# Experts' pass: tokens and silu product transposed in 32x32 blocks on VectorE, with the product moved through DRAM

## The reference, cut to what matters

```python
logits = x @ gate_weight.T                      # 4096 tokens, 64 experts
scores = softmax(logits); topk_w, topk_idx = top_k(scores, 8); topk_w = topk_w / sum(topk_w)
sorted_tokens = repeat(x, 8)[argsort(flat_ids)]           # 32768 rows
g = ragged_dot(sorted_tokens, w_gate, group_sizes)        # 1024 -> 384
u = ragged_dot(sorted_tokens, w_up, group_sizes)          # 1024 -> 384
out = ragged_dot(silu(g) * u, w_down, group_sizes)        # 384 -> 1024
y = sum(out[inv].reshape(-1, 8, 1024) * topk_w[:, :, None], axis=1)
```

## Time and profile before

| | |
|---|---|
| median of 3 runs | 6763.86 us (6763.16 to 6765.04) |
| profiled execution | 6763.85 us, its span 6762.0 us |
| granted TensorE clock, mean | 0.992 |
| TensorE busy over the span | 6614.3 us, 98% |
| DVE, ACT, POOL busy | 3302.4, 2933.3, 1147.4 us |
| DMA packets, bytes | 733960, 1048.19 MB |
| tiles of the experts' pass; expert weight loads in it | 287; 63 of each kind |

### The profile page before, as it was taken

One profiled execution on the slowest core, in us unless ns is written; L12 is line 12 of the kernel. 1 busy time (PEld: TensorE's weight loads), 2 busy tenths in 40 slices (PEclk: granted clock), 3 DMA queues, 4 the chain that ended last, 5 costly groups with the idle time before them and its releaser, 6 DMA issues.

```text
span 6762.0 us, 107799 instructions
## 1 busy us (share of the span) xinstructions
PE 6614.3 (98%) x34530; PEld 5884.0 (87%) x34531; DVE 3302.4 (49%) x4252; ACT 2933.3 (43%) x3606; POOL 1147.4 (17%) x1015
## 2 busy tenths in 40 slices
PE   9999998999999999699999999999999999999998
PEld 7888887887888788599989999999999999999998
DVE  4443324999999899732443334322422323323333
ACT  3321224888888644432443334322422333333333
POOL 1000000000000155511211211111111212111121
PEclk9999999999999999899999999999999999999999
DMA  8853555555555666455676566654644556556555
GB/s 257 231 197 143 155 143 145 129 127 128 128 129 128 182 171 171 128 156 130 178 211 172 152 174 189 160 137 106 186 106 106 134 134 162 148 147 162 155 153 152
DMA packets 733960, 1048.19 MB, mean 155 GB/s; under 512 B 301281, under 2 KB 531425, under 8 KB 733858
## 3 DMA queue, kind: packets, MB, share of 16 engines
q0 software_dynamic: 109792, 368.12, 23.5%
q1 hardware_dynamic: 467680, 381.55, 22.1%
q10 hardware_dynamic: 156386, 297.29, 13.0%
HBM read 724.43 MB, written 322.31 MB: 155 GB/s over the span
## 4 chain that ended last, share of the span: by engine, by line
PE 51%; DMA 4%; issue 1%; ACT 1%; DVE 1%; ACTq 0%; SPq 0%; POOLq 0%; DVEq 0%
PE moe_ps_y L1332 5%; PE moe_ps_gate L1345 5%; PE moe_ps_gate L1346 5%; PE moe_ps_gate L1347 5%; PE moe_ps_up L1347 5%; PE moe_ps_up L1346 5%; PE moe_ps_up L1345 5%; PE moe_ps_y L1334 5%; PE moe_ps_y L1333 5%; DMA out<-moe_y,moe_rec_s 2%; PE moe_ps_xT L1322 2%; PE moe_ps_hT L1353 1%; DMA moe_rec_s<-table 1%; DMA first_raw<-in_w_up 1%; ACT moe_gu_hi L1375 0%
## 5 line engine op out<-in xcount | busy, mean ns | idle before, releaser
L1449 DVE SCALAR_TENSOR_TENSOR moe_hidden<-moe_silu,moe_rec_w,moe_ps_up 128x384 f32<-128x384 f32 x286 | 175.8, 615 | 1384.6 <-PE moe_ps_up L1347 1190.3
L1345 PE MATMUL moe_ps_gate<-moe_gu_hi,moe_xT_hi 128*128 128x384 f32 x2288 | 793.4, 347 | 11.1 <-DVE moe_xT_lo L1442 7.5
L1300 POOL DMA_INDIRECT out<-moe_y,moe_rec_s x287 | 478.2, 1666 | 1909.9 <-DMA moe_rec_s<-table 1037.5
L1346 PE MATMUL moe_ps_gate<-moe_gu_lo,moe_xT_hi 128*128 128x384 f32 x2288 | 768.1, 336 | 0.0
L1347 PE MATMUL moe_ps_gate<-moe_gu_hi,moe_xT_lo 128*128 128x384 f32 x2288 | 767.8, 336 | 0.0
L1347 PE MATMUL moe_ps_up<-moe_gu_hi,moe_xT_lo 128*128 128x384 f32 x2288 | 765.1, 334 | 0.0
L1345 PE MATMUL moe_ps_up<-moe_gu_hi,moe_xT_hi 128*128 128x384 f32 x2288 | 764.2, 334 | 0.0
L1346 PE MATMUL moe_ps_up<-moe_gu_lo,moe_xT_hi 128*128 128x384 f32 x2288 | 764.2, 334 | 0.0
L1332 PE MATMUL moe_ps_y<-moe_d_hi,moe_hT_hi 128*128 128x512 f32 x1722 | 696.5, 404 | 3.0 <-DVE moe_hT_lo L1455 3.0
L1334 PE MATMUL moe_ps_y<-moe_d_hi,moe_hT_lo 128*128 128x512 f32 x1722 | 677.2, 393 | 0.0
L1333 PE MATMUL moe_ps_y<-moe_d_lo,moe_hT_hi 128*128 128x512 f32 x1722 | 669.6, 389 | 0.0
(11 more groups left out here) (202 smaller groups left out, 13975.2 us busy)
## 6 DMA issues: line engine op xcount, KB each, us to landing
first_raw<-in_w_gate ACTq DMA_DIRECT2D x63, 1536.0 KB, 9.6
first_raw<-in_w_up ACTq DMA_DIRECT2D x63, 1536.0 KB, 14.7
moe_raw_d<-in_w_down ACTq DMA_DIRECT2D x63, 1536.0 KB, 7.1
proj_a_raw<-in_ctxT POOLq DMA_DIRECT2D x64, 512.0 KB, 5.1
kst<-proj_o SPq DMA_DIRECT2D x256, 128.0 KB, 2.7
vst<-proj_o SPq DMA_DIRECT2D x64, 512.0 KB, 2.6
qst<-proj_o SPq DMA_DIRECT2D x256, 128.0 KB, 2.2
att_kt<-kst SPq DMA_DIRECT2D x64, 512.0 KB, 3.6
```

The source lines that it names most:

```text
L1300: nc.gpsimd.indirect_dma_start(out=acc[:, :], out_offset=bass.IndirectOffsetOnAxis(ap=rec_s[:].bitcast(I32)[:, 0:1], axis=0), in_=y[:], in ...
L1345: nc.tensor.matmul(o[:, 0:I], xT_hi[:, c], gu_hi[:, b, k, c], start=(c == 0), stop=False)
L1346: nc.tensor.matmul(o[:, 0:I], xT_hi[:, c], gu_lo[:, b, k, c], start=False, stop=False)
```

## The change

TensorE's transposes go. In their place:
- The output pass writes the features of `h2st` in another order, by quarters (`by_quarter`), and the gate table is loaded to match, in 8 pieces of 32 partitions.
- `rec_g` is loaded four times (one DMA per 32 partitions), POOL makes row numbers of quarter rows from it (`rows`), and four indirect DMAs fetch 1 KB quarters, such that VectorE's transpose in 32x32 blocks (`turn_tokens`, into PSUM) leaves the tokens of t+2 transposed. Gathers run one tile further ahead.
- `hidden` is stored to DRAM (`hst`) and loaded back with four DMAs in another order (`hidden_g`), and DVE transposes it in blocks (`turn_hidden`). The rows of w_down are loaded to match, by four DMAs for each expert.
- DVE's eight splits of gate and up stand in two halves, with `turn_hidden` between them. SP's list has another order. ACT's `tokens_high` waits for gate and up of the tile before, which share its buffer.

The diff, cut to its core:

```diff
+W = 32
+G = P // W
 ...
+def grouped(rows, s):
+    n = rows.shape[1] // G
+    return rows[:, s * n:(s + 1) * n, :].rearrange("o (j a) i -> a (o j) i", a=W)
 ...
+def in_chunks(rows):
+
+    return rows.rearrange("p (j s a) -> p j s a", s=G, a=W)
+
+
+def by_quarter(rows):
+
+    return rows.rearrange("p (s j a) -> p j s a", s=G, a=W)
 ...
-                for dst, src in ((gamma_sb, row_broadcast(gamma, H)), (beta_sb, row_broadcast(beta, H)),
-                                 (gate_sb, gateT.rearrange("(c p) e -> p c e", p=P))):
+                for dst, src in ((gamma_sb, row_broadcast(gamma, H)), (beta_sb, row_broadcast(beta, H))):
                     pool.dma_start(dst[:], src).then_inc(consts_in, 16)
+                gate_rows = gateT.rearrange("(c s a) e -> c a s e", s=G, a=W)
+                for c in range(C):
+                    rows = slice(c % G * W, (c % G + 1) * W)
+                    pool.dma_start(gate_sb[rows].rearrange("a (s h) e -> a h s e", s=G)[:, c // G], gate_rows[c]).then_inc(consts_in, 16)
 ...
-                        nc.scalar.activation(h2[:, 1 - b], x1[:, 1 - b], ACT.Identity, bias=shift[:],
+                        nc.scalar.activation(by_quarter(h2[:, 1 - b]), in_chunks(x1[:, 1 - b]), ACT.Identity, bias=shift[:],
                                              scale=rstd[:, 1]).then_inc(h2_done, 1)
 ...
-        tokens, xT_hi, xT_lo = s.sb("tokens", [P, H], F32R), s.sb("xT_hi", [P, C, P], F32R), s.sb("xT_lo", [P, C, P], F32R)
+        tokens, xT_hi, xT_lo = s.sb("tokens", [P, H]), s.sb("xT_hi", [P, C, P], F32R), s.sb("xT_lo", [P, C, P], F32R)
 ...
+        rec_g, rec_w, rec_s = s.sb("rec_g", [P, G, 2]), s.sb("rec_w", [P, 2]), s.sb("rec_s", [P, 2])
+        group, rows = s.sb("group", [P, 1]), s.sb("rows", [P, G], I32)
+        hidden_g = s.sb("hidden_g", [P, G, I // G])
+        gate_ps, up_ps, hT_ps = s.ps("gate", [P, HALF]), s.ps("up", [P, HALF]), s.ps("hT", [P, G * P])
+        turned, y_ps = s.ps("turned", [P, H]), s.ps("y", [P, H])
+        xT_ps = turned[:].rearrange("p (g j b) -> p j g b", g=G, b=W)
+        hT_t = hT_ps[:, 0:I]
+        hT_v = hT_t.rearrange("p (g j b) -> p j g b", g=G, b=W)
+
+        def by_group(tile):
+            return tile[:].rearrange("p j (g b) -> p j g b", b=W)
 ...
+        h2_quarters = h2st.rearrange("t (s n) -> (t s) n", s=G)
 ...
+                def record_groups(rows):
+                    for k in range(G):
+                        sp.dma_start(rec_g[k * W:(k + 1) * W], rows.rearrange("(g b) w -> b g w", b=W)).then_inc(rec_g_in, 16)
+
+                record_groups(table[REGION:REGION + P, :])
 ...
+                for k in range(G):
+                    sp.dma_start(raw_d[k * W:(k + 1) * W], grouped(w_down[0:1], k)).then_inc(raw_in[2], 16)
 ...
                 def tile(t, is_first=False):
+                    sp.wait_ge(hidden_done, t + 2)
+                    sp.wait_ge(hidden_in, 16 * G * (t + 1))
+                    sp.sem_inc(sp_passed, 1)
+                    sp.dma_start(hst[:, :], hidden[:]).then_inc(hidden_stored, 16)
+                    record(rec_w, t + 1, rec_w_in)
                     if not is_first:
                         sp.wait_ge(added, 16 * t)
                     sp.sem_inc(sp_passed, 1)
                     record(rec_s, t - 1, rec_s_in)
-                    sp.wait_ge(hidden_done, t + 2)
+                    sp.wait_ge(hidden_stored, 16 * (t + 2))
+                    sp.wait_ge(hT_done, t + 1)
                     sp.sem_inc(sp_passed, 1)
-                    record(rec_w, t + 1, rec_w_in)
-                    sp.wait_ge(gathered, 16 * (t + 3))
+                    for k in range(G):
+                        part = hst[:, k * (I // G):(k + 1) * (I // G)].rearrange("(g b) n -> b g n", b=W)
+                        sp.dma_start(hidden_g[k * W:(k + 1) * W], part).then_inc(hidden_in, 16)
+                    sp.wait_ge(rows_done, t + 4)
                     sp.sem_inc(sp_passed, 1)
-                    record(rec_g, t + 3, rec_g_in)
+                    record_groups(record_rows(t + 4))
 ...
-                    pool.wait_ge(rec_g_in, 16 * (t + 1))
-                    pool.wait_ge(xT_done, t)
+                    pool.wait_ge(rec_g_in, 16 * G * (t + 1))
+                    pool.wait_ge(turned_done, t)
                     pool.sem_inc(pool_passed, 1)
-                    nc.gpsimd.indirect_dma_start(
-                        out=f32(tokens[:]), out_offset=None, in_=h2st[:, :],
-                        in_offset=bass.IndirectOffsetOnAxis(ap=rec_g[:].bitcast(I32)[:, 0:1], axis=0)).then_inc(gathered, 16)
+                    nc.gpsimd.tensor_scalar(rows[:], rec_g[:].bitcast(I32)[:, :, 0], float(G), group[:], ALU.mult, ALU.add).then_inc(rows_done, 1)
+                    pool.wait_ge(rows_done, t + 1)
+                    pool.sem_inc(pool_passed, 1)
+                    for g in range(G):
+                        nc.gpsimd.indirect_dma_start(
+                            out=tokens[:, g * (H // G):(g + 1) * (H // G)], out_offset=None, in_=h2_quarters,
+                            in_offset=bass.IndirectOffsetOnAxis(ap=rows[:, g:g + 1], axis=0)).then_inc(gathered, 16)
 ...
+                gather(2)
                 with pool.Fori(0, last_tile + 1) as t:
-                    gather(t + 2)
+                    gather(t + 3)
                     add(t - 1)
 ...
-                def transpose_tokens(t):
-                    pe.wait_ge(gathered, 16 * (t + 1))
-                    for c in range(C):
-                        last = nc.tensor.transpose(xT_r[:, c], tokens[:, c * P:(c + 1) * P], ident_r[:])
-                    last.then_inc(xT_done, 1)
 ...
-                    transpose_tokens(t + 1)
                     down(t - 1, b_before)
-                    pe.wait_ge(hidden_done, t + 2)
-                    for c in range(CI):
-                        last = nc.tensor.transpose(hT_ps[:, c], hidden[:, c * P:(c + 1) * P], ident[:])
-                    last.then_inc(hT_done, 1)
                     if e is not None:
                         pe.wait_ge(w_lo_done, PIECES * e + PIECES)
 
-                transpose_tokens(0)
 ...
                 def tokens_high(t):
-                    act.wait_ge(xT_done, t + 1)
-                    nc.scalar.copy(xT_hi[:], xT_ps).then_inc(xT_hi_done, 1)
+                    act.wait_ge(turned_done, t + 1)
+                    if not (isinstance(t, int) and t == 0):
+                        act.wait_ge(gu_done, 2 * t)
+                    nc.scalar.copy(by_group(xT_hi), xT_ps).then_inc(xT_hi_done, 1)
 ...
-                    act.dma_start(raw_d[:], w_down[bass.ds(e, 1)].rearrange("o (c p) i -> p (o c) i", p=P)).then_inc(raw_in[2], 16)
+                    for s in range(G):
+                        act.dma_start(raw_d[s * W:(s + 1) * W], grouped(w_down[bass.ds(e, 1)], s)).then_inc(raw_in[2], 16)
 ...
                     act.wait_ge(hT_done, t + 2)
-                    nc.scalar.copy(hT_hi[:], hT_ps).then_inc(hT_hi_done, 1)
+                    nc.scalar.copy(by_group(hT_hi), hT_v).then_inc(hT_hi_done, 1)
 ...
                 def tokens_low(t):
                     dve.wait_ge(xT_hi_done, t + 1)
-                    nc.vector.tensor_tensor(xT_lo[:], xT_ps, f32(xT_hi[:]), ALU.subtract).then_inc(xT_lo_done, 1)
+                    nc.vector.tensor_tensor(by_group(xT_lo), xT_ps, f32(by_group(xT_hi)), ALU.subtract).then_inc(xT_lo_done, 1)
+
+                def turn_tokens(t):
+                    dve.wait_ge(gathered, 16 * G * (t + 1))
+                    if not (isinstance(t, int) and t == 0):
+                        dve.wait_ge(xT_lo_done, t)
+                    nc.vector.transpose(turned[:], tokens[:]).then_inc(turned_done, 1)
+
+                def turn_hidden(t):
+                    dve.wait_ge(hidden_in, 16 * G * (t + 2))
+                    dve.wait_ge(hT_lo_done, t + 1)
+                    nc.vector.transpose(hT_t, hidden_g[:].rearrange("p g n -> p (g n)")).then_inc(hT_done, 1)
 
                 def tile(t, e=None, b=None):
                     dve.wait_ge(silu_done, t + 1)
                     dve.wait_ge(gu_done, 2 * t + 2)
-                    dve.wait_ge(hT_done, t + 1)
+                    dve.wait_ge(hidden_stored, 16 * (t + 1))
                     dve.wait_ge(rec_w_in, 16 * (t + 1))
                     nc.vector.scalar_tensor_tensor(out=hidden[:], in0=silu[:], scalar=rec_w[:, 1:2], in1=up_ps[:, 0:I],
                                                    op0=ALU.mult, op1=ALU.mult).then_inc(hidden_done, 1)
                     tokens_low(t + 1)
+                    turn_tokens(t + 2)
                     if e is not None:
-                        split(e, b, 0, GU)
+                        split(e, b, 0, GU // 2)
+                    turn_hidden(t)
+                    if e is not None:
+                        split(e, b, GU // 2, GU)
                     dve.wait_ge(hT_hi_done, t + 1)
```

(4 more changed lines are left out.)

52 lines of the change are left out of this document (24 added, 28 removed).

## The result

| | before | after |
|---|---|---|
| median, range | 6764.45 us, 6763.16 to 6767.01 | 7408.72 us, 7403.17 to 7412.49 |
| span of the profiled execution | 6762.0 us | 7401.6 us |
| granted TensorE clock, mean | 0.992 | 0.947 |

The changed kernel is slower: ratio 1.0951, 95% interval 1.0933 to 1.0968 (four executions of each). The prediction had 6965 us and a range to 7190, so it had the side right and was 444 us too low.

What follows compares the result with a forecast made beforehand. The prediction took TensorE's queue to bound the experts' pass (busy 3877.41 of 3917 us). From 6763.9 us it took 278 for removed transposes and added 479 for waits around 63 weight loads: 6965 us, range 6650 to 7190.

Steps and rivals of the forecast that it cites:

- b: Down product after an expert's first tile: hT_lo comes late, TensorE waits 2.0 us per weight load (0.5 to 3.5).
- c: Second tile of an expert: store and loads of `hidden` land late beside weight loads, delaying down by 2.0 us (1 to 4).
- What is removed: TensorE's token and product transposes and the lateness behind them: 0.97 us saved a tile, 278 us (253 to 298).
- What lies beside TensorE: Added work off TensorE: DVE transposes of 1.15 and 0.5 us, four POOL gathers holding 5.1 us, more SP and ACT transfers.
- Bytes hardly grow: DMA traffic of the added stores, loads and gathers: claimed to hardly grow in bytes.
- The ordinary tile: Tile without weight loads, 12.52 us: the product's trip over two tiles ends at 31.8, wanted at 33.4, 1.6 us to spare.
- a: First tile of an expert: w_down splits and loads delay silu and xT_lo; 4.1 us worked out, 3.6 taken (1.5 to 5).
- The clock: TensorE in the experts' pass: read at a granted clock of 1.00, the 2.4 GHz level; no slow work was added.
- Rival 1: Faster: the product's path is 2.5 us shorter; a, b and c shrink to 3.0 us in all; 6675 us, chance 0.25.
- Rival 2: The path exceeds TensorE's work in every tile, 1.1 us too many in each of 161 tiles; 7142 us, chance 0.12.
- Rival 3: Four turns: beside weights each of four `hidden` loads waits 6.1 us, c is 6.5 us; 7248 us, chance 0.07.

Runs made afterwards that it cites:

- e10: Changed kernel, but SP stores the product, waits, and stores it again before it is loaded: 7736.14 us.
- e5: Changed kernel, but ACT issues the w_down loads in the next expert's first tile, behind silu and the tokens' high part: 7229.78 us.
- e6: Changed kernel, but SP loads the product back before it waits for the sum of t-2 and loads rec_s: 7415.64 us.
- e12: Changed kernel, the product stored only once, in the very first tile; loads bring that old product to every tile, so the output differs: 7304.54 us.
- e13: Changed kernel with e12 and e6 together, neither store nor sum ahead of the product's loads; output is e12's: 7060.88 us.
- e3: Changed kernel without the weight loads of experts 1 to 63; all compute with expert 0's weights, splits stay: 6830.45 us.

## Why the prediction was right or wrong

**The miss in its own terms.** 6965 had 278 saved and 479 lost. Measured are 294 saved, 641 lost by waits and 292 by slow work behind them: 162 + 292 - 16 = 438 us of the 444; the profiled execution lies 6 us under the median. So two steps failed. The slow work is a term that the sum put at nothing, without a reason. And down's waits, b and c together, were priced at 252 us and are 375.3. With the waits as measured and no slow work the time would have been 7127 us, inside the range.

**What is removed: right.** 1.03 us a tile for 0.97. The lateness of the product after each transpose went too, nearly all of the 1.04.

**What lies beside TensorE: nearly right.** DVE's transposes take 1.26 and 0.59 us for 1.15 and 0.5. The gathers start 1.27 us apart, as forecast from the earlier trace rows. "Bytes hardly grow" was wrong: 114 MB more, in 349 thousand more packets.

**The ordinary tile: right.** Forecast were the sum at 6.1 us into the tile and hT_lo ended at 6.8. In the tile from 4295.29 the sum is issued at 4301.40, at 6.1, and hT_lo ends at 4302.48, at 7.2, with 1.2 us to spare instead of 1.6. What the forecast of this tile lacks is the product's own loop of one tile, which has 1.5 us to spare here and which e10 closes.

**a: the mechanism right, the total by luck.** Forecast were the splits' end at 10.7, silu at 13.8 and the next gate product at 16.6 if all of it holds; the rows have 11.2, 14.6 and 17.3. I then took 3.6 for the 4.1 that was worked out, on the ground that ACT can read w_down earlier. The reason helped nothing, since silu stands behind ACTq's loads, which stand behind DVE's splits. Here a is 4.85 us, 4.70 of them the wait. Over all experts the gate products' waits for xT_lo are 267.0 us less the 40.0 at the start of the pass, 227 in all, and 3.6 x 63 is 227. That is luck: 57 experts have a second tile, and there the wait is 4.0 us, the 4.1 that was worked out. Behind the six experts of one tile the gate product waits for splits instead, 35.7 us in all, which was not forecast. e5 confirms the path: with the load moved, first tiles are 3.4 us shorter.

**b: the wait low, the tile wrong.** In this expert down waits 1.74 us for a forecast of 2.0; over all it waits 163 us in 57 second tiles, 2.9 each. And this tile is 4.9 us too long, since its gate product runs at half clock behind a's wait, 2.7 us.

**c: the term that was mis-sized most.** The prediction put the store's and the loads' lateness on down's wait with 2.0 us. Measured are 212 us in 56 waits, 3.8 each. In this expert the third tile is 8.5 us too long: down waits 5.89 and then runs slowly. "The store and the loads of `hidden` fall into that stretch and land 2 to 4 us late each" was right singly (loads 6.01 us for 1.98). Wrong was to price them as one delay on a path with some spare. In this expert nothing was spare, and down waited until 4356.82 for the trip. And there are two ways to the product's loads, the store's landing and the gathers with the sum, that both stretch beside weight loads. e6, e12 and e13 show it: +7, -104, -348.

**The clock: the step that failed.** The earlier trace rows had 1.00, and I priced every wait at its own length. The rows show TensorE at 0.50, the 1.2 GHz level, after the waits of 4.70 and 5.89 us, and at 1.00 later in the same tile. The 292 us are a reading of rows; no run separates the clock from the waits. Yet it goes with them: TensorE is busy 3673.80 us in e3 at a mean of 0.98, 3766.37 in e13 at 0.95, 3874.90 here at 0.92, with the same 18894 matmuls. By the count above the slow work is a third of the added idle time in e3 (90 for 270 us) and not quite half in e13 (183 for 401) and here.

**The rivals.** Rival 1 (faster) falls: a, b and c did not shrink. Rival 2 (every tile) falls too: quiet tiles stay at 12.467. e10 shows that a store more is enough to bring a wait in every tile about, from an expert's sixth on. Rival 3 comes nearest in time and has the place right, the second tile's product beside the loads, and in this expert the end too: the product's last packet ends at 4354.38, 0.66 us behind the last of the gate and up loads, at 4353.72. What it has wrong is the count of turns, for the four loads land together, 6.0 us after the last issue, and what they wait beside, since POOL's packets hold most of the last 4 us. Of the rule of the Trainium skill ("DMA: Bandwidth & Descriptors", queues, rings and completion order), that an engine takes turns between its queues, the rows show the direction: packets of queues 0, 1 and 10 pass side by side from 4350.20 on, and the same loads land after 1.98 us and after 6.01. That it is this rule which makes them late, no run here shows.

**Still open.** Of the 387 us that the order of waits costs without any loads, no run here shows how much falls to the splits and how much to the gathers, nor what ACT's order of `y` and hT_hi costs. A second buffer for `hidden` and `hidden_g`, that would let the trip start a tile earlier, was not tried.

## What to carry to other kernels

Before a transpose leaves the matmul engine for a trip through DRAM, count all ways that join in front of the trip's last transfer, and price them beside the heaviest traffic, not in a quiet stretch: the loop that fits there with 1.2 us to spare failed here wherever weights were loaded. Where TensorE was never idle, price new waits at their length and a third to a half as much again for slow work behind the long ones (641 and 292 us here; the wait of 1.74 us had none). Split a change with two parts before judging it: here the token half is worth 1.6% once the waits around it are reordered, and the product half alone costs 477 us.
